# Middle stage of a two-layer kernel: the low-rank rows turned one product earlier, and the third chunk's gate set behind the fourth chunk's values

## The reference, cut to what matters

```python
x = x + s * g                          # s: output projection of the first attention, g: first gate
xn = _layernorm(x, axis=-1)
q = xn @ wq.T ; k = xn @ wk.T          # 32 + 8 heads of 16, then the rotary embedding on both
v = xn @ wv.T
router_logits = xn @ Wr.T + br         # 8 experts of the low-rank branch
scores = 8 * softmax(router_logits)
low = xn @ A.T                         # 8 experts x 16 = 128 columns
out = einsum('bshr,hor,bsh->bso', low, B, scores)
g = silu(2 * out)                      # the second gate, read at the very end of the kernel
```

## Time and profile before

| | us |
|---|---|
| median of 3 runs | 2365.8 |
| lowest, highest | 2361.75, 2368.64 |
| the profiled execution | 2369.5 |
| its span | 2367.7 |
| PE, DVE, ACT, POOL busy in the span | 87%, 63%, 46%, 33% |
| the middle stage, PE's first product to the next stage's first product | 1371.3 to 1664.1 |

### The profile page before, as it was taken

How to read it: one execution, slowest core, us unless ns; L and a number is a source line. 1 busy time by engine, 2 the same in 40 slices (tenths; PEclk the granted TensorE clock), 3 DMA queues, 4 the chain that set the end, 5 groups by cost and what they waited for, 6 DMA issues and landing times. The chain is left out here.

```text
span 2367.7 us, 46673 instructions
## 1 busy us (share of the span) xinstructions
PE 2058.6 (87%) x19128; PEld 1009.8 (43%) x19128; DVE 1489.3 (63%) x2992; ACT 1100.8 (46%) x1987; POOL 771.9 (33%) x735
## 2 busy tenths in 40 slices
PE   7999989998647898979999789987588888888878
PEld 3444435555213333445555434443244444443434
DVE  3534354443559999716777725445888888888813
ACT  1212135555324333227777502324277777777760
POOL 0102212222447456504444402223343333433310
PEclk9999999999879899989999989997799999999999
DMA  6120101101412121362222264132936455364424
GB/s 240 36 89 36 67 19 32 32 14 44 140 43 83 54 67 32 107 208 75 90 82 76 76 175 143 58 79 76 216 59 84 69 72 81 58 89 65 59 79 142
DMA packets 149338, 198.03 MB, mean 84 GB/s; under 512 B 57154, under 2 KB 85956, under 8 KB 146564
## 3 DMA queue, kind: packets, MB, share of 16 engines
q1 hardware_dynamic: 147540, 181.41, 30.9%
q10 hardware_dynamic: 1584, 13.63, 1.6%
HBM read 134.69 MB, written 60.29 MB: 82 GB/s over the span
## 5 line engine op out<-in xcount | busy, mean ns | idle before, releaser
L3112 DVE TENSOR_REDUCE f_chunk_max<-f_ps_a 128x64 f32<-128x1024 f32 x320 | 319.7, 1033 | 47.4 <-PE f_ps_a L2856 25.0
L2985 ACT ACTIVATE conv_in<-f_ps_s 128x512 f32<-128x512 f32 x480 | 258.5, 602 | 86.6 <-PE f_ps_s L2887 42.7
L2856 PE MATMUL f_ps_a<-conv_in 128*32 128x512 bf16 (+3 forms) x3072 | 201.0, 340 | 42.1 <-DVE f_chunk_max L3112 25.4
L2078 ACT ACTIVATE d_probs<-d_ps_s,d_shift 128x512 f32<-128x512 f32 (+3 forms) x384 | 196.7, 584 | 82.7 <-PE d_ps_s L2017 72.8
L2887 PE MATMUL f_ps_s<-f_qs,f_ks 128*32 128x512 bf16 x2304 | 208.3, 382 | 23.3 <-ACT f_qs L2976 14.7
L1420 PE MATMUL c_ps_c<-conv_in,c_wT 128*128 128x512 f16 x768 | 186.2, 402 | 18.5 <-DVE c_odd L1721 14.1
L3052 POOL TENSOR_SCALAR f_absent<-f_rest 128x576 f32<-128x576 f32 x32 | 54.4, 1700 | 304.9 <-DVE f_rest L3129 180.7
L2909 PE MATMUL f_ps_o<-conv_in,f_v 128*32 128x512 f32 (+2 forms) x1152 | 125.9, 522 | 28.3 <-ACT conv_in L2985 27.4
L2976 ACT ACTIVATE f_qs<-f_ps_s 32x512 bf16<-32x512 f32 x192 | 112.8, 587 | 75.6 <-PE f_ps_s L2870 73.3
L2028 PE MATMUL d_ps_o<-d_probs,conv_in 128*64 128x512 f32 (+3 forms) x768 | 146.1, 488 | 0.0
L2856 PEld LDWEIGHTS f_ps_a<-conv_in 128*32 128x32 bf16 x3072 | 71.8, 98 | 164.3 <-DVE f_chunk_max L3112 68.6
(11 more groups left out here) (364 smaller groups left out, 4451.5 us busy)
## 6 DMA issues: line engine op xcount, KB each, us to landing
conv_in<-qk SPq DMA_DIRECT2D x96, 128.0 KB, 4.0
f_qs<-qk SPq DMA_DIRECT2D x96, 128.0 KB, 4.8
conv_in<-q_parts SPq DMA_DIRECT2D x8, 1024.0 KB, 5.1
o0T<-d_stage SPq DMA_DIRECT2D x16, 512.0 KB, 3.2
conv_in<-o0T SPq DMA_DIRECT2D x4, 2048.0 KB, 10.6
qk<-e_part SPq DMA_DIRECT2D x12, 640.0 KB, 4.9
f_qs<-qk SPq DMA_DIRECT2D x96, 64.0 KB, 4.7
rows<-in_qc_w ACTq DMA_DIRECT2D x3, 1536.0 KB, 7.0
```

Of the source, the lines that this page charges most:

```text
L2078: act.activation(probs[n % RING][SCORES[c][1]][:, lo:hi], ps_s[c % BANKS][:, lo - hi + CH:], ACT.Exp, bias=shift[:, 0:1], scale=HD0 ** -0. ...
L2856: last = pe.matmul(out[side(e), h, 0:w], qa[u][:, 2 * p + h, side(e, qt * P)], ka[u][:, kh * CH:kh * CH + w], start=True, stop=not last_keys)
L2985: act.activation(probs[m % HELD][:, :, at:at + P], bank_of["s", i, n][:].rearrange("p (h n) -> p h n", n=P), ACT.Exp, scale=HD1 ** -0.5).t ...
L3112: dve.tensor_reduce(chunk_max[:, qt - 2, :, at:at + w // CHUNK], src.rearrange("p h (c k) -> p h c k", k=CHUNK), AX.X, ALU.max).then_inc(a ...
```

## The change

Three things are moved; no instruction is added or removed.

1. In every chunk PE's turn of the weighted rows stands ahead of product 4 in place of behind it.
2. In every chunk ACT copies it to `weightedT` behind the first `mids`, ahead of raw copy 4. Before, that copy stood between `mids(2)` and `highs(4)`.
3. gates(2) leaves the end of chunk 2. On PE it stands in rest(3), behind the values of chunk 3 and ahead of product 0; on ACT behind the four `tok` copies of chunk 3 and ahead of raw copy 0. The waits that share the banks `ps_y` follow: the values of chunk 3 wait for the Silu of chunk 1 only, and gates(2) waits for the `tok` copies of chunk 3.

```diff
-                pe.wait_ge(gate_ready, TT * (c + 1))
+                pe.wait_ge(gate_ready, TT * (c + 1 if c < NCH - 1 else c))
                 for t in range(TT):
...
                     last.then_inc(tok_done, 1)
+                if c == NCH - 1:
+                    gates(c - 1)
                 for i in range(NQK):
+                    if i == NQK - 1:
+                        turn_weighted(c)
                     pe.wait_ge(raw_ready, NQK * c + max(i - 1, 0) + 2)
...
                     last.then_inc(qk_done, 1)
+
+            def turn_weighted(c):
                 pe.wait_ge(soft_step, SOFT * (c + 1))
...
             def gates(c):
                 pe.wait_ge(wT_ready, c + 2)
-                pe.wait_ge(tok_ready, TT * (c + 1))
+                pe.wait_ge(tok_ready, TT * (c + 1 if c != NCH - 2 else NCH))
...
                 if c + 2 < NCH:
                     project(c + 2)
-                gates(c)
+                    gates(c)
             rest(NCH - 1)
             gates(NCH - 1)
...
                     act.activation(tok[:, t, :], ps_y[t % 2][:, 0:TOK], ACT.Copy).then_inc(tok_ready, 1)
+                if c == NCH - 1:
+                    gates(c - 1)
...
                     if i >= 3:
                         mids(i - 3)
+                    if i == NQK - 2:
+                        act.wait_ge(wT_done, c + 1)
+                        act.activation(weightedT[:], ps_t[0][:], ACT.Copy).then_inc(wT_ready, 1)
                 highs(NQK - 2)
                 mids(NQK - 3)
-                act.wait_ge(wT_done, c + 1)
-                act.activation(weightedT[:], ps_t[0][:], ACT.Copy).then_inc(wT_ready, 1)
                 highs(NQK - 1)
                 mids(NQK - 2)
                 mids(NQK - 1)
+                if c != NCH - 2:
+                    gates(c)
+
+            def gates(c):
                 act.wait_ge(gate_stored, 16 * (c + 1))
```

## The result

The changed kernel took 2370.06 us (median of 22 runs, 2361.61 to 2379.17), the kernel before 2364.7 us (22 runs, 2356.97 to 2369.41). The ratio is 1.0025, 95% interval 1.0013 to 1.0037: 5.9 us slower, between 3.1 and 8.7 (the two medians differ by 5.4). That is +0.25%, against a forecast of +0.23% (2371.3 us, +5.5). All ratios leave out two executions that ran slow from end to end, one of the kernel before (2561 us) and the profiled one of the kernel with 44 unused products (4317 us), whose trace is therefore not used.

The account below looks back on a forecast made before the run. In chunk 3 whatever delays product 0 was taken to delay the stage's end, the earlier idle time being set by DVE's xn. Terms 0 + 5.49 + 0 + 0 + 0 + 0 = +5.5 on 2365.8 gave 2371.3 us, range 2365.5 to 2376.5.

Parts of the forecast that it names:

- gates(2) leaves the hole: End of chunk 2: removing gates(2) from PE's 20.3 us idle stretch, ended by DVE's xn, saves nothing, 0 us.
- gates(2) ahead of product 0: Chunk 3 on PE: the 4.86 us block starts at 1625.51 and delays product 0 from 1624.88 to 1630.37, +5.49 us.
- It passes on in full: Chunk 3's rotation on POOL, DVE and ACT has no slack, so the whole 5.49 us delays the stage's end.
- The turn ahead of product 4: Every chunk: product 4 and raw copy 4 come at most 0.60 us later, covered by existing waits, 0 us.
- a wait other than 2.49 us in project(2): Sign of being wrong: PE's wait in project(2) in the changed kernel's profile differs from 2.49 us.
- The copy `weightedT` earlier: ACT's part copies: it delayed nothing, since highs(4) waited for DVE's sum; 0 us, bounds -0.6 and 0.
- gates(3) at the end: Stage end: last pair at low clock, store issued 1.80 us later but covered by faster landing; 0 us, uncovered +1.8.
- The clock: Chunk 3 after PE's longer idle time: transposes start cold before and after, 0 us; bound +3.4, or +1.8 at the block.
- values at the low clock: Sign of being wrong: chunk 3's values or products run at clock 0.50 beyond what they had before.
- the low clock rival: Chunk 3's values or product 0 run cold: +3.4 or +1.8 us on top of 5.5, likeliest 2374.7 us; chance 0.22.

Follow-up runs that it names:

- the kernel with 44 unused products: Changed kernel plus 44 unused products in PE's idle time ahead of chunk 3's transposes, which they overran; ratio 1.0082 against the kernel before.
- the turn alone: Kernel before with the earlier turn and the earlier weightedT copy, gates(2) staying at the end of chunk 2; ratio 0.9998.
- the point alone: Kernel before with only gates(2) moved behind chunk 3's values, turn and weightedT copy where they were; ratio 1.0025.
- four banks: Changed kernel with gates(2)'s third and fourth products written to project's two banks, so PE skips the wait inside the block; ratio 1.0009 against the kernel before.
- a filler: Changed kernel plus 21 unused products (18.2 us) in PE's 20.3 us idle time ahead of chunk 3's transposes; ratio 1.0028 against the kernel before.
- the second trace of before: Kernel before, unchanged, profiled again; this execution took 2367.0 us.

## Why the prediction was right

- *gates(2) leaves the hole, 0 us.* Right. PE idles 20.28 us, `xn` ends the hole in either case, and a stage with the turn alone waits the same 4.98 us for it.
- *gates(2) ahead of product 0, +5.49 us.* Right. 5.7 us in the traces (the block 4.95 us where I took 4.86 from gates(1), and 0.10 us more of wait at its start: 1617.49 is 0.14 us behind the end of the `tok` copy at 1617.35, where I took 0.04), and the point alone gives the whole ratio. The length of the block is what counts, as four banks show in the trace.
- *It passes on in full.* Right: 39.2 us from product 0 to the next stage, in the first traces before and after (39.21 and 39.35 in the second ones).
- *The turn ahead of product 4, 0 us.* Nearly. I looked for a delay and counted what covers it, and gave chunk 0 the same answer. There the delay moved a POOL instruction off a DVE one, -0.6 us. The prediction names a wait other than 2.49 us in project(2) as a sign of being wrong, and this one came.
- *The copy `weightedT` earlier, 0 us.* Right, for the reason given: `highs(4)` starts when DVE's sum ends, in the changed kernel too.
- *gates(3) at the end, 0 us.* Right. The last pair took 3.78 us after 9.84 us of idle time, and the store landed in at most 4.4 us. That cover is not safe in every execution: in the trace of four banks the same store took up to 5.8 us, and the stage paid 1.5 us.
- *The clock, 0 us.* The size holds, the reason doesn't, and that is luck. I read one trace, in which the clock rose during the transposes, and set it against the rule of the Trainium skill ("TensorE: Matmul & The Clock Gate", "Part 4: PE-mode transpose") that transposes do not count as activity that brings the full clock. Among the eleven traces that one is alone. In seven, the clock stood at 0.50 through chunk 3's transposes and came back only among the values, as in the first trace of the changed kernel (the transposes, then the values in two stretches):

```profile
1603.15:1606.99 3.84, 3.84 (x16) 2.92 (x16) 0.00 (x0) 1.79 (x3) 0.00 (x0) 0.50 0.00 0
1607.68:1611.50 3.82, 3.82 (x9) 3.00 (x10) 0.00 (x0) 0.00 (x0) 0.00 (x0) 0.50 0.00 0
1611.50:1616.92 5.42, 5.42 (x25) 4.29 (x23) 0.00 (x0) 1.17 (x3) 0.00 (x0) 1.00 0.00 0
```

  In the other three it fell during the transposes, as at 1601.5 after a filler at the full clock and 2.28 us of idle time. In chunk 2 of the second trace of before it fell at about 1562, just behind transposes and 0.69 us of idle time. The rows lean to the rule, though the first trace stands against its strict form, and 31 of the 36 chunks 0 to 2 of the twelve traces kept 7.39 us of values behind the same transposes. So a second sign of being wrong came, values at the low clock (9.24 us, where the first trace of before has 7.39). It did not cost the forecast anything, as far as traces tell, because the kernel before mostly pays for it as well: with gates(2) at its old place and no filler, five of six traces have values of 9.07 to 9.63 us. I had taken the sixth, its first, for its ordinary state. The cost of the low clock rival was there on both sides, 1.9 to 2.1 us where I had priced 3.4.

The spread of the low clock is also why two single profiles could not show the change: 6.2 us above the lowest in one trace of the stage, 3.2 in the other.

## What to carry to other kernels

Work that stands in another engine's wait is free where it is; before moving it, ask what follows it in the new place, and whether the wait that it leaves had any other end. Compare two profiles of one kernel before a difference of a few microseconds between two kernels is read from them, and take off what the clock did. Here the gap was shortened from what ended it, the POOL clearing that held `xn`, and not by taking work out of it.

## What the runs showed of the hardware

- A run of transposes does not always hold the full clock: with PE busy on transposes 3.7 us and idle 0.69 us, the values behind them took 9.07 us in place of 7.39 in chunk 2 of the second trace of before, with a mean clock of 0.54 over their first 3.64 us. The same happened in chunk 0 of four other traces, and in 31 of 36 such chunks it did not.
- DVE's subtraction of two SBUF tiles takes 0.68 us alone and 1.75 us when a POOL product has started just ahead of it. Delaying the POOL instruction by 0.44 us shortened the whole chain by 0.6 us.
- DVE's `xn` of four instructions takes 1.91 us, and 5.96 us when a POOL memset of 3.51 us starts 0.08 us after it and one of 1.11 us follows: the first instruction takes 3.88 us in place of 0.54, and the second lasts until behind the second memset. The same section of the Trainium skill as above states that `tensor_scalar` can run in a mode that takes both pairs of ports, and that whichever of DVE and GpSimd comes second then waits for the whole of the other's instruction. The sizes agree (3.88 us against 0.08 + 3.51, and the rest of its own), the order not quite: DVE's row starts first, and it is DVE that waits. Which mode DVE was in, no row shows.
